# A third table of blocks in a mixture-of-experts kernel with routing on the chip

## What is computed

```python
x = x + tanh(g_xattn) * attention(layernorm(x), ctx, ctx, mask, Wq, Wk, Wv, Wo, heads=16)
h = layernorm(x)
shared = silu(h @ Sg.T) * (h @ Su.T) @ Sd.T
probs = sigmoid(h @ router.T + bias)              # 8 experts
scores, idx = top_k(probs, 2); scores /= scores.sum(-1)
combined = sum over the 2 chosen e of scores_e * (silu(h @ G[e]) * (h @ U[e])) @ D[e]
x = x + tanh(g_ffn) * (shared + combined)
```

## Time and profile before

| | us |
|---|---|
| median of 3 runs (175.99 to 176.20) | 176.14 |
| the profiled execution | 176.26 |
| its span (first to last record) | 174.4 |
| TensorE busy | 159.9 (92%) |
| VectorE busy | 127.6 (73%) |
| ScalarE busy | 111.3 (64%) |
| GpSimd busy | 110.0 (63%) |

### The profile page before, as it was taken

The page is one execution under the profiler, slowest core; times in us unless marked ns, Lnnn a source line. Parts: engine busy times, 40 slices in busy tenths (PEclk is TensorE's granted clock), DMA queues, the critical chain, the costliest instruction groups (busy, mean ns, idle before and its releaser), DMA issues.

```text
span 174.4 us, 4611 instructions
## 1 busy us (share of the span) xinstructions
PE 159.9 (92%) x1412; PEld 139.5 (80%) x1412; DVE 127.6 (73%) x612; ACT 111.3 (64%) x427; POOL 110.0 (63%) x139
## 2 busy tenths in 40 slices
PE   7799889999999999999999996997899999999970
PEld 7687669998898998898998875895677788887860
DVE  2689988665989597878597978478784777776283
ACT  3666997774868774868774968651665566665300
POOL 3675799854869744768724768567644566666621
PEclk9999999999999999999999999999999999999997
DMA  5899996730000000000000000001414223211172
GB/s 164 267 368 379 414 401 241 284 136 4 15 2 0 19 2 4 31 17 19 31 4 0 16 21 16 17 26 40 109 40 118 64 78 83 67 52 41 53 244 91
DMA packets 11096, 17.35 MB, mean 99 GB/s; under 512 B 2075, under 2 KB 6945, under 8 KB 10944
## 3 DMA queue, kind: packets, MB, share of 16 engines
q1 hardware_dynamic: 9504, 14.59, 24.3%
q0 software_dynamic: 1280, 2.20, 3.9%
q10 hardware_dynamic: 288, 0.26, 0.4%
HBM read 9.99 MB, written 7.51 MB: 100 GB/s over the span
## 4 chain that ended last, share of the span: by engine, by line
PE 47%; POOL 14%; ACT 14%; issue 12%; DMA 6%; DVE 4%; SPq 1%; DVEq 0%; POOLq 0%
ACT probs L727 8%; PE misc L411 8%; POOL ys L1449 7%; PE pt L385 5%; PE o_bank L400 5%; PE s_even L374 5%; PE proj_q L331 3%; DMA wq_raw<-wqT 3%; PE proj_k L331 3%; PE proj_k L333 3%; PE proj_k L332 3%; PE proj_q L333 2%; PE proj_q L332 2%; DMA probs<-ys 2%; POOL xs L1369 2%
## 5 line engine op out<-in xcount | busy, mean ns | idle before, releaser
L727 ACT ACTIVATE probs<-probs,negmax 128x128 f32<-128x128 f32 x128 | 49.9, 393 | 18.8 <-DVE negmax L937 18.7
L1339 POOL TENSOR_TENSOR probs<-probs,rinv 128x512 f32<-128x512 f32 x32 | 33.0, 1047 | 19.6 <-DVE rinv L951 19.5
L1449 POOL DMA_INDIRECT ys<-probsT,places x23 | 22.5, 979 | 15.0 <-ACT places L852 12.9
L727 ACT ACTIVATION_READ_ACCUMULATOR probs<-probs,negmax 128x1 f32 x128 | 24.2, 189 | 0.0
L937 DVE CUSTOM_DVE_ANT_0 probs<-s_even,mask 128x128 f32<-128x128 f32 x64 | 18.1, 283 | 5.2 <-issue 5.2
L1369 POOL DMA_INDIRECT xs<-xrow,slot x16 | 16.3, 1021 | 6.8 <-issue 3.9
L385 PE MATMUL pt<-ident_sb,probs 128*128 128x128 f32 x128 | 17.6, 277 | 1.7 <-POOL probs L1339 1.1
L374 PE MATMUL s_even<-kT,qT 64*128 64x128 f32 x128 | 18.5, 284 | 0.4 <-DVE negmax L937 0.4
L374 PE MATMUL s_odd<-kT,qT 64*128 64x128 f32 x128 | 18.5, 285 | 0.0
L374 PEld LDWEIGHTS s_even<-kT,qT 64*128 64x128 f32 x128 | 15.4, 187 | 3.5 <-issue 1.2
L937 DVE CUSTOM_DVE_ANT_0 probs<-s_odd,mask 128x128 f32<-128x128 f32 x64 | 18.1, 283 | 0.0
(11 more groups left out here) (282 smaller groups left out, 454.8 us busy)
## 6 DMA issues: line engine op xcount, KB each, us to landing
xs<-pad SPq DMA_DIRECT2D x5, 858.0 KB, 6.6
xg<-xs SPq DMA_DIRECT2D x23, 66.0 KB, 1.9
down_sb<-down SPq DMA_DIRECT2D x1, 1152.0 KB, 9.7
probs<-ys SPq DMA_DIRECT2D x4, 256.0 KB, 3.9
gu_raw<-gu SPq DMA_DIRECT2D x3, 256.0 KB, 5.8
wk_raw<-wkT SPq DMA_DIRECT2D x2, 256.0 KB, 4.0
wq_raw<-wqT SPq DMA_DIRECT2D x2, 256.0 KB, 5.0
mask<-mask SPq DMA_DIRECT2D x8, 64.0 KB, 1.9
```

The costliest lines, as they stand in the source:

```text
L727: e = act.activation(probs[:, r, l, :], probs[:, r, l, :], ACT.Exp, bias=negmax[:, r, l:l + 1], scale=-1.0, accum_out=rowsum[:, r, l:l + 1])
L1339: pool.tensor_tensor(quad, quad, rinv[:, r, 4 * u:4 * u + 4].unsqueeze(2).to_broadcast([P, 4, P]), ALU.mult).then_inc(norm_done, 1)
L1449: pool.indirect_dma_start(out=ys, out_offset=bass.IndirectOffsetOnAxis(ap=places[:, n:n + 1].bitcast(U32), axis=0), in_=y_sb[n % IN_FLIGHT ...
```

## The change

A third table, made of the counts after batch 6, stands between the two. STAGES names the rounds after which a table is made (2, 3, 4), SEEN the batches that have been counted by then (6, 7, 8), STARTS the first block of each table (0, 5, 7): so the first table lists 5 blocks, the middle one 2 (blocks 5 and 6), the last the rest. The middle table takes full blocks that are not early; then its two are added to the early ones. The scattered rows have three semaphores, so blocks 5 and 6 are fetched after the scatters of batch 6. On TensorE the ranks of batch 6 get three matmuls for the counts. On VectorE two steps of the middle table stand ahead of the choice for batch 7, the others between block 1's remainders and the last table, of which two steps and not three stand ahead of block_hidden(0). The shared expert's pass stays ahead of block 5 (UNIT_AT), the quota steps at n = 10 (QUOTA_AT).

```diff
-SEEN = 6
-EARLY = (SEEN * P * TOP_K - E_ROUTED * (P - 1)) // P + 1
+STAGES = (2, 3, LAST)
+SEEN = [ROUTED[r][-1] + 1 for r in STAGES]
+STARTS = [0] + [(seen * P * TOP_K - E_ROUTED * (P - 1)) // P + 1 for seen in SEEN[:-1]]
...
+UNIT_AT = 1
+
+QUOTA_AT = 10
...
-            sp.wait_ge(table_ready, 1)
-            found = [find(n) for n in range(EARLY)]
-            sp.wait_ge(scattered[0], 16 * SEEN * TOP_K)
-            for n in range(EARLY):
-                gather(n, found[n])
-            sp.wait_ge(table_ready, 2)
-            found += [find(n) for n in range(EARLY, IN_FLIGHT)]
-            sp.wait_ge(scattered[1], 16 * (B - SEEN) * TOP_K)
-            for n in range(EARLY, IN_FLIGHT):
-                gather(n, found[n])
+            landed = [16 * TOP_K * (end - start) for start, end in zip([0] + SEEN, SEEN)]
+            for stage, start, end in zip(range(3), STARTS, STARTS[1:] + [IN_FLIGHT]):
+                sp.wait_ge(table_ready, stage + 1)
+                found = {n: find(n) for n in range(start, end)}
+                sp.wait_ge(scattered[stage], landed[stage])
+                for n in range(start, end):
+                    gather(n, found[n])
...
-                if r in (2, LAST):
+                if r in STAGES:
                     count = route_bank[r][:, cnt_cols]
...
-                if n + 2 == EARLY:
+                if n + 2 == STARTS[UNIT_AT]:
...
-            def table_steps(late):
-
-                n = 6 * late
+            def table_steps(stage):
+
+                n = (0, 6, 13)[stage]
                 by_expert = "p (e j) -> p e j"
-                bank = route_bank[LAST if late else 2]
-                count = bank[:, cnt_cols].unsqueeze(2).to_broadcast([P, E_ROUTED, ROWS])
-                dve.wait_ge(rk_done, LAST + 1 if late else 3)
-                if late:
+                count = route_bank[STAGES[stage]][:, cnt_cols].unsqueeze(2).to_broadcast([P, E_ROUTED, ROWS])
+                dve.wait_ge(rk_done, STAGES[stage] + 1)
+                if stage < 2:
+                    dve.scalar_tensor_tensor(full[:].rearrange(by_expert, e=E_ROUTED), count, 0.5 - P, edges.rearrange(by_expert, e=E_ROUTED),
+                                             ALU.add, ALU.is_gt).then_inc(counts_read, 1)
+                else:
...
+                yield
+                dve.wait_ge(counts_read, stage + 1)
+                present = exists if stage == 2 else full
+                if stage:
+                    dve.tensor_tensor(present[:], present[:], early[:], ALU.subtract).then_inc(table_step, 1)
                     yield
...
+                if stage == 2:
+                    dve.memset(carrier[:, 0:1], 0.0).then_inc(table_step, 1)
+                else:
+                    first = (early, full)[stage]
+                    dve.scalar_tensor_tensor(first[:], upto[:], float(STARTS[stage + 1] - STARTS[stage]), full[:],
+                                             ALU.is_le, ALU.mult).then_inc(table_step, 1)
                     yield
...
                 dve.wait_ge(table_step, n + 4)
-                dve.tensor_reduce(table_f[late][:, 0:1], below[:], AX, ALU.add).then_inc(table_step, 1)
+                if stage == 1:
+                    dve.tensor_tensor(early[:], early[:], full[:], ALU.add).then_inc(table_step, 1)
+                dve.tensor_reduce(table_f[stage][:, 0:1], below[:], AX, ALU.add).then_inc(table_step, 1)
...
+            middle_table = table_steps(1)
+            run(middle_table, 2)
             finish(choose_steps(LAST))
             block_lo(0)
             finish(weight_steps(LAST))
             place(LAST)
             block_lo(1)
-            last_table = table_steps(1)
-            run(last_table, 3)
+            finish(middle_table)
+            last_table = table_steps(2)
+            run(last_table, 2)
             block_hidden(0)
...
-                                            in_=xrow[:, b, k, :], in_offset=None).then_inc(scattered[b >= SEEN], 16)
+                                            in_=xrow[:, b, k, :], in_offset=None).then_inc(scattered[(b >= SEEN[0]) + (b >= SEEN[1])], 16)
```

More of the change, by code:

```diff
@@ L133, in build @@
         full, early = sb("full", [P, CANDIDATES]), sb("early", [P, CANDIDATES])
-        table_f, table = ([sb(f"{n}{i}", [P, 2], t) for i in range(2)] for n, t in (("table_f", F32), ("table", I32)))
+        table_f, table = ([sb(f"{n}{i}", [P, 2], t) for i in range(3)] for n, t in (("table_f", F32), ("table", I32)))
         xg = [sb(f"xg{i}", [P, WIDTH]) for i in range(IN_FLIGHT)]
@@ L165, in build @@
         in_down = sem("in_down")
-        scattered = [sem("scattered0"), sem("scattered1")]
+        scattered = [sem(f"scattered{i}") for i in range(3)]
         in_xg = [sem(f"in_xg{i}") for i in range(IN_FLIGHT)]
@@ L221, in build, with stage_of, table_row @@
         y_of = y_rows.rearrange("p (b k) h -> p b k h", k=TOP_K)
+        def stage_of(n):
+            return sum(n >= start for start in STARTS) - 1
+        def table_row(n):
+            stage = stage_of(n)
+            return table[stage][n - STARTS[stage]:n - STARTS[stage] + 1, :]
         def load_y(engine, n):
@@ L287, in find @@
             def find(n):
-                late = n >= EARLY
-                row = n - EARLY * late
-                return sp.value_load(table[late][row:row + 1, 0:1]).with_bounds(min_val=0, max_val=CANDIDATES)
+                return sp.value_load(table_row(n)[:, 0:1]).with_bounds(min_val=0, max_val=CANDIDATES)
             def gather(n, c):
@@ L591, in block_expert @@
             def block_expert(n):
[L592 to L596, removed]
+                if n in STARTS[1:]:
+                    pe.wait_ge(table_ready, stage_of(n) + 1)
+                return pe.value_load(table_row(n)[:, 1:2]).with_bounds(min_val=0, max_val=E_ROUTED)
             def stay_warm(times):
@@ L1074, in table_steps @@
                     dve.memset(table_f[0][:], 0.0).then_inc(table_step, 1)
-                present = exists if late else full
                 dve.wait_ge(table_step, n + 1)
@@ L1081, in table_steps @@
                 yield
-                if not late:
-                    dve.scalar_tensor_tensor(early[:], upto[:], float(EARLY), full[:], ALU.is_le, ALU.mult).then_inc(table_step, 1)
+                if stage == 2:
[4 more added lines that the diff above has]
+                                             ALU.is_le, ALU.mult).then_inc(table_step, 1)
                     yield
-                else:
-                    dve.memset(carrier[:, 0:1], 0.0).then_inc(table_step, 1)
                 dve.wait_ge(table_step, n + 4)
-                dve.tensor_reduce(table_f[late][:, 0:1], below[:], AX, ALU.add).then_inc(table_step, 1)
+                if stage == 1:
+                    dve.tensor_tensor(early[:], early[:], full[:], ALU.add).then_inc(table_step, 1)
+                dve.tensor_reduce(table_f[stage][:, 0:1], below[:], AX, ALU.add).then_inc(table_step, 1)
                 yield
-                dve.tensor_reduce(table_f[late][:, 1:2], below[:].rearrange(by_expert, e=E_ROUTED)[:, :, ROWS - 1], AX,
+                dve.tensor_reduce(table_f[stage][:, 1:2], below[:].rearrange(by_expert, e=E_ROUTED)[:, :, ROWS - 1], AX,
                                   ALU.add).then_inc(table_step, 1)
-                dve.wait_ge(table_step, n + 6)
-                dve.tensor_copy(table[late][:], table_f[late][:]).then_inc(table_ready, 1)
+                dve.wait_ge(table_step, n + (6, 7, 6)[stage])
+                dve.tensor_copy(table[stage][:], table_f[stage][:]).then_inc(table_ready, 1)
             def quota_steps():
-                beyond = float(IN_FLIGHT * FEWEST - EARLY) + 0.5
+                beyond = float(IN_FLIGHT * FEWEST - STARTS[-1]) + 0.5
                 dve.tensor_scalar(more[:], iota_sb, beyond, upto[:, CANDIDATES - 1:], ALU.add, ALU.is_le).then_inc(quota_ready, 1)
@@ L1276, in _ @@
                 run(last_table, 1)
-                if n + 1 == EARLY:
+                if n + 1 == STARTS[UNIT_AT]:
                     hidden(1)
-                if n == 2 * EARLY:
+                if n == QUOTA_AT:
                     quota = quota_steps()
-                if n >= 2 * EARLY:
+                if n >= QUOTA_AT:
                     run(quota, 1)
```

7 lines of the change are left out of this document (removed).

## The result

The changed kernel is slower: 177.31 us, the median of 4 runs (177.21 to 177.41), against 176.06 for the kernel before on the same chip (4 runs, 175.82 to 176.20). The ratio is 1.0072, 95% interval 1.0055 to 1.0090. The profiled execution took 177.35 us against 176.26, so 1.09 more, and its span is 175.5 us against 174.4.

What follows compares the result with a forecast made beforehand. TensorE was taken to bound the kernel: 176.14 us median, plus 1.40 of TensorE idle time, 0 for the fetch and 0 for hidden steps, gave 177.54, forecast as 177.5. The 8-in-10 range was 176.7 to 178.3.

Steps and rivals of the forecast that it cites:

- What bounds the loop: Loop over 23 blocks: it runs at TensorE's speed, scatters follow results, and idle time added from block 0 reaches the end.
- The fetch at 0: Block 5's transpose: fetching rows some 2 us earlier gains 0, since the shared expert's pass covers the fetch.
- The bound of 0.21: Block 5's transpose: the most the earlier fetch could save, the 0.21 us its weight load waits for rows.
- The hidden steps at 0: Ahead of batch 7's choice: two table steps (0.51 us) fit 0.81 us of VectorE idle time; count matmuls 0, at most 0.1.
- The finish at 1.50: VectorE between block 1's remainders and the last table: the rest of the middle table takes 1.50 us, bounds 1.25 to 1.65.
- the lower bound of 1.25: Rest of the middle table: 1.25 us if its compare is not lengthened beside a scatter, giving a time of 177.3.
- The scan given back at 0.21: Last table: its scan moves behind block 0's hidden product, returning 0.21 us, so the product starts 1.29 us later.
- TensorE's step at block 0: Block 0's hidden transpose: released by block 0's product, so the whole 1.29 us go into TensorE.
- The second meeting at block 1's down product: Block 1's down product: VectorE's copy is 1.50 us late, less 0.25 of room, so TensorE starts about 1.4 late.
- Partly paid back: Rival: TensorE's waits of 0.21, 0.20 and 0.37 us close, the delay shrinks to 0.62, time 176.8; chance 0.10.
- Faster: Rival at block 5's transpose: a fetch normally landing 2 us later holds TensorE, the change removes that, 175.7; chance 0.05.
- Slower by the clock: Rival: TensorE's longer standstill drops its granted clock to 1.2 GHz, up to 1.4 us more per block, 179 to 181; chance 0.05.

Runs made afterwards that it cites:

- e5: The kernel before, with two useless VectorE operations (0.5 us) ahead of block 0's hidden product and no third table; ratio 1.0023 to the kernel before.
- e6: The kernel before, with four useless VectorE operations (1.0 us) ahead of block 0's hidden product and no third table; 177.17 us, ratio 1.0042.
- e2: The changed kernel, with blocks 5 and 6 fetched only once the last table and all scattered rows are there; ratio 1.0057 to the kernel before.
- e7: The kernel before, with the shared expert's pass moved from ahead of block 5's transpose to ahead of block 7's; 178.24 us, ratio 1.0110.
- e3: The changed kernel, with block 0's hidden product ahead of the middle table's rest and the last table's first two steps; 179.4 us, ratio 1.0169.
- e11: The kernel before, with eight useless VectorE operations (2.0 us) ahead of block 0's hidden product; executions of 178.06 to 179.56 us, ratio 1.0122.

## Why the prediction was right

The forecast was 177.5 us, 1.40 above the kernel before; measured were 177.31 and 1.25, in the profiled runs 1.09. The mechanism was right, and the sizes in it came out too high: the profiled runs give 0.31 us less than the forecast. That the medians are within 0.2 us of it is in part luck. Step by step:

- **What bounds the loop.** Right. Scatters follow results and results follow TensorE. Most of a delay put in at block 0 arrives at block 20 (e5, e6: 0.41 of 0.49, 0.86 of 1.00), though the chain of waits names the scatters.
- **The fetch at 0.** Right, by e2, and the reason (the pass of the shared expert covers it) by e7. The bound of 0.21 was not needed.
- **The hidden steps at 0.** Right for VectorE's two steps, which took 0.40 us (122.04 to 122.44) and not 0.51. The three count matmuls cost 0.08, inside the bound of 0.1, but the reason for taking 0 was wrong: the cover named was VectorE's idle time, and the path goes past VectorE, from the logits through ScalarE's load to block 0's remainders.
- **The finish at 1.50.** Mis-sized: 1.28 (125.39 to 126.67), next to the lower bound of 1.25. The term that failed is the compare. I kept the 0.51 us of the earlier trace rows; here it took 0.25, though it started together with a scatter of GpSimd, which took 0.96. The step behind the mark of the first two then comes 0.25 us after it (125.87 to 126.12), where it was 0.40 in the first table (116.78 to 117.18), and the add takes 0.15 and not 0.20:

```profile
125.70 0.25 DVE L1084 TENSOR_SCALAR below<-upto,partition_f 128x64 f32<-128x64 f32 x1
125.70 0.96 POOL L1380 DMA_INDIRECT xs<-xrow,slot  x1 [0.99 <-DVE slot L1056]
125.87 0.22 DVE L1090 SCALAR_TENSOR_TENSOR full<-upto,full 128x64 f32<-128x64 f32 x1
126.12 0.22 DVE L1095 TENSOR_TENSOR early<-early,full 128x64 f32<-128x64 f32 x1
126.27 0.21 DVE L1096 TENSOR_REDUCE table_f<-below 128x1 f32<-128x64 f32 x1
```

The Trainium skill, SBUF — State Buffer, section SBUF: two separate sides, says that the shared pair of ports is an exclusive lock, held for a whole instruction by a GpSimd operation or by one of VectorE in a mode with two ports. Read as the prediction read it, for any overlap of compare and scatter, one of the two should have been longer; the trace does not agree in this place. It is what the prediction had for that case: 1.25 and 177.3. What the profiles show is narrower. In 11 of the 14 the first table's compare starts 0.63 to 0.65 us behind the start of a scatter, and takes 0.51 us, the scatter 1.16. In the other three (e2, e3, e7) it starts 0.70 or 0.71 behind, and they take 0.31 or 0.32 and 1.03. All other compares take 0.24 to 0.28, those too that start 0.71 to 0.81 behind a later scatter. The middle table's compare starts with its scatter.

- **The scan given back at 0.21.** Mis-sized the other way: 0.33. From the last table's comparison to the product it was 0.72 us (125.28 to 126.00) and is 0.39 (126.67 to 127.06). The scan had to wait for the subtraction, and started 0.26 us behind it; the product doesn't, and starts 0.14 behind it.
- **TensorE's step at block 0.** Right: the product is what releases it. 1.06 us in place of 1.29, which is 0.11 (0.08 of matmuls, 0.03 by which this profile lay later already) + 1.28 - 0.33.
- **The second meeting at block 1's down product.** Right as a mechanism. TensorE waits for VectorE there (the copy ends at 130.67, the product starts at 130.82), but the copy is 1.12 us late and not 1.50. That is 0.23 less from the steps above, and 0.15 less since the scan, now behind the product, makes VectorE only 0.06 us later between the product and this copy (1.06 to 1.12), and not 0.21. The product is 1.01 late in place of 1.40, and what follows it 1.10. This step sets the delay of the loop: at block 0's down product 0.2 us had been paid back (129.13 after 128.24, so 0.89 late), and here they are lost again.
- **The rivals.** Partly paid back: not by block 20. The waits of the earlier trace rows are there again, as 0.21 and 0.37 us, and the 0.2 us paid back at block 0's down product are lost at block 1's. Faster: it needed a fetch that lands late, and e7 made one; there the third table is worth something, here not. Slower by the clock: not in the changed kernel, whose windows from 124 to 138 us show 1.00, but e11 and e3 show the mechanism behind waits of 1.9 us.

Between the profiled difference (1.09) and that of the medians (1.25) lie 0.16 us that no row of mine explains.

## What to carry to other kernels

Before an earlier fetch is bought, look at the engine that uses it: a wait on a weight load costs nothing where the matmuls around it keep their pitch. Then lay the new work out in the written order of its engine and ask, for each operation that it pushes back, who is released by it; small operations ahead of the one on which the bounding engine waits are paid nearly in full (0.86 of 1.00 us here), and the same operations spread further on cost less (0.23 in place of 0.97 us), as long as they don't hold the next operation that it wants. Idle time in front of an operation is cover only for work that is not ahead of what the operation itself waits for.

## What the runs showed of the hardware

A wait of TensorE can have a second price. The waits of 0.79 us (changed kernel) and 1.06 us (e7, where the weight load waited 1.25) left the granted clock at 1.00 in the profiled executions. Those of 1.9 us in e3 and e11 were followed by some 3 us at 0.50, which is 1.2 GHz. The fall came after the work had gone on, in e3 about 0.6 us after and in e11 about 1.8. In e11 that cost 1.5 us on top of the 2.0 put in. The Trainium skill, TensorE: Matmul & The Clock Gate, Part 1, gives the gate two states, full rate when busy and half rate after idleness; the rows agree on the two levels. What decides these runs don't show, and the length of the wait alone does not seem to: two of e11's four executions were 1.4 us faster, with a mean clock of 0.997 or more.

The same compare of 128x64 took 0.51 us in the first table and 0.25 in the middle one, each beside a scatter of GpSimd. Over the 14 profiles it was long only in the first table, 0.51 us where it started 0.63 to 0.65 us into the scatter and 0.31 or 0.32 where it started 0.70 or 0.71 into it. The scatter was longer with it (1.16 and 1.03 us, where it took 0.96 to 1.01 beside the short ones). So the two are long together there, and less so with a shift of some 0.07 us. No experiment moved the compare on purpose, so this is a pattern and its cause is not shown.
